# Which engine scales the first corner of the interpolated tiles while the next image's offsets are computed

## The reference, cut to what matters

```python
def _modulated_dcn(x, w_off, b_off, w):
    om = conv(x, w_off) + b_off          # 27 channels: 18 offsets, 9 masks
    ...
    v = samp(y0, x0) * ((1 - ly) * (1 - lx))[:, None] + samp(y0, x0 + 1) * ((1 - ly) * lx)[:, None] \
        + samp(y0 + 1, x0) * (ly * (1 - lx))[:, None] + samp(y0 + 1, x0 + 1) * (ly * lx)[:, None]
    v = v * mask[:, None]
    return jnp.einsum('bckhw,ock->bohw', v, w.reshape(w.shape[0], C, KK))
```

## Time and profile before

| | |
|---|---|
| median of 3 runs | 5400.81 us (5400.7 to 5404.68) |
| profiled execution, its own time | 5390.38 us |
| its span | 5388.6 us |
| granted TensorE clock, mean | 0.972 of full speed |
| TensorE matmul busy | 4889.6 us |
| VectorE busy | 4392.5 us |
| ScalarE busy | 2297.6 us |
| GpSimd busy | 2282.9 us |

### The profile page before, as it was taken

One profiled execution on the slowest core, in us unless ns is written; L12 is line 12 of the kernel. 1 busy time (PEld: TensorE's weight loads), 2 busy tenths in 40 slices (PEclk: granted clock), 3 DMA queues, 4 the chain that ended last, 5 costly groups with the idle time before them and its releaser, 6 DMA issues. The chain is left out here.

```text
span 5388.6 us, 80437 instructions
## 1 busy us (share of the span) xinstructions
PE 4889.6 (91%) x26816; PEld 2678.9 (50%) x26816; DVE 4392.5 (82%) x11212; ACT 2297.6 (43%) x5430; POOL 2282.9 (42%) x2311
## 2 busy tenths in 40 slices
PE   7868999999989998999989999899998989988888
PEld 4435554555545555455544555445554555544443
DVE  5656888878887888878888788888888878898998
ACT  2234444344443443534445344343444444443554
POOL 0003444444453444434444444444444344454776
PEclk9979999999999999999999999999999999999999
DMA  4326778877798777977779777887778877788999
GB/s 162 122 93 208 271 248 291 304 250 264 247 318 285 251 266 245 337 269 259 257 251 338 250 258 256 277 315 250 275 254 292 297 252 263 251 305 308 387 398 353
DMA packets 493125, 1451.51 MB, mean 269 GB/s; under 512 B 47396, under 2 KB 117420, under 8 KB 492460
## 3 DMA queue, kind: packets, MB, share of 16 engines
q0 software_dynamic: 331776, 1208.11, 64.3%
q1 hardware_dynamic: 160940, 238.27, 12.6%
HBM read 1309.60 MB, written 136.59 MB: 268 GB/s over the span
## 5 line engine op out<-in xcount | busy, mean ns | idle before, releaser
L730 POOL DMA_INDIRECT G<-table,IDX x2304 | 2282.0, 990 | 3066.6 <-DVE V L1381 2269.6
L749 PE MATMUL ps<-VT,s_wconv 128*128 128x512 f32 x4608 | 2277.5, 618 | 39.7 <-DVE R L1165 39.7
L1381 DVE SCALAR_TENSOR_TENSOR V<-G,WT,V 128x256 f32<-128x256 f32 x4608 | 2019.1, 479 | 122.6 <-DVE V L1381 3.2
L1109 ACT ACTIVATE VT<-ps 128x512 f32<-128x512 f32 x1152 | 686.0, 595 | 2390.0 <-PE ps L955 2387.9
L749 PEld LDWEIGHTS ps<-VT,s_wconv 128*128 128x128 f32 x4608 | 828.7, 194 | 871.7 <-issue 836.1
L1374 DVE SCALAR_TENSOR_TENSOR V<-G,WT 128x256 f32<-128x256 f32 x2304 | 1006.5, 477 | 84.0 <-ACT G L1098 40.1
L1129 DVE TENSOR_TENSOR E<-ps,s_band 128x512 f32<-128x512 f32 x1024 | 649.5, 682 | 455.3 <-PE ps L811 273.3
L955 PEld LDWEIGHTS ps<-s_ident,V 128*128 128x128 f32 x4608 | 574.5, 143 | 755.8 <-issue 754.5
L1098 ACT ACTIVATE G<-G,WT 128x256 f32<-128x256 f32 x1850 | 841.2, 499 | 111.0 <-DMA G<-table,IDX 110.1
L955 PE MATMUL ps<-s_ident,V 128*128 128x128 f32 x4608 | 708.8, 277 | 86.4 <-DVE V L1381 84.4
L787 PE MATMUL ps<-XN,s_wqk 128*128 128x512 f32 x1024 | 490.1, 606 | 14.8 <-ACT XN L1011 14.6
(11 more groups left out here) (101 smaller groups left out, 2764.9 us busy)
## 6 DMA issues: line engine op xcount, KB each, us to landing
table<-E SPq DMA_DIRECT2D x384, 176.0 KB
G<-table,IDX POOLq DMA_INDIRECT x2304
X<-in_x SPq DMA_DIRECT2D x64, 512.0 KB, 7.3
x<-X SPq DMA_DIRECT2D x64, 512.0 KB, 7.0
R<-x SPq DMA_DIRECT2D x64, 512.0 KB
out<-R SPq DMA_DIRECT2D x64, 512.0 KB, 5.8
G<-in_x SPq DMA_DIRECT2D x56, 512.0 KB, 4.4
s_wconv<-in_wconv SPq DMA_DIRECT2D x1, 2304.0 KB, 9.2
```

What stands on the lines that cost most here:

```text
L730: e.indirect_dma_start(G[a % NG][:, :], None, T[b % 2], bass.IndirectOffsetOnAxis(ap=IDX[b % 2][:, col:col + 1], axis=0)).then_inc(d_g[a % ...
L749: mm = e.matmul(CV[oh][:, :], s_wconv[:, h, t, oh * P:(oh + 1) * P], VT[U % 2][:, h, :], start=(t == 0 and h == 0), stop=(t == 8 and h == 1))
L1109: e.activation(VT[U % 2][:, :, 2 * P * pair:2 * P * (pair + 1)], BK[banks.place[use]][:, :].rearrange("p (h n) -> p h n", h=2), ACT.Copy). ...
L1381: e.scalar_tensor_tensor(vt[:, :], gt[:, q * C:(q + 1) * C], wt[:, col, q:q + 1], vt[:, :], ALU.mult, ALU.add).then_inc(lerp[q - 1], 1)
```

## The change

Every "scale" step is ScalarE's. The flag, the state that set it and the count of scales by engine go, as does VectorE's multiply with its semaphore. VectorE's first lerp waits for ScalarE's count alone.

```diff
     def front(b):
-        offsets_run[0] = False
         yield from layer0(b)
-        offsets_run[0] = True
         yield from offset_phase(b)
-        offsets_run[0] = False
...
         def scale(m):
             if m < PAIRS:
-                steps.append(("scale", b, m, not offsets_run[0]))
+                steps.append(("scale", b, m))
...
-                elif kind == "scale" and s[3]:
+                elif kind == "scale":
                     b, m = s[1:3]
...
                     for a, gt, vt, col in pairs:
-                        if not scaled[a][0]:
-                            e.wait_ge(d_g[a % NG], 16 * (a // NG + 1))
-                            if u % 9 == 0 and pair == 0:
-                                e.wait_ge(wts, WTS * (b * NCH + c + 1))
-                            e.tensor_scalar(gt[:, 0:C], gt[:, 0:C], wt[:, col, 0:1], None, ALU.mult).then_inc(dve_scale, 1)
                     if M > 2:
                         e.wait_ge(*filled(("vt", M - 3)))
...
                     for a, gt, vt, col in pairs:
-                        on_act, count = scaled[a]
-                        if on_act:
-                            e.wait_ge(act_scale, count)
-                        else:
-                            e.wait_ge(dve_scale, count)
+                        e.wait_ge(act_scale, a + 1)
                         e.scalar_tensor_tensor(vt[:, :], gt[:, C:2 * C], wt[:, col, 1:2], gt[:, 0:C],
                                                ALU.mult, ALU.add).then_inc(lerp[0], 1)
```

More of the change, by code:

```diff
@@ L88, in order_of_steps @@
     have_kv, have_logits, have_x1 = set(), set(), set()
-    offsets_run = [False]
     def hop(n):
@@ L402, in runs @@
     return [(0, slot, n)] + ([(n, 0, 4 - n)] if n < 4 else [])
[L405 to L414, removed]
 def build(nc, x, wqk, wv, wn, wkx, bkg, alpha, beta, wproj, woff, boff, wconv,
@@ L421, in build @@
     banks, prods = rotations(steps)
-    scaled = scale_counts(steps)
     ctx = ExitStack()
@@ L530, in build @@
         wts = sem("wts")
-        dve_scale = sem("dve_scale")
         lerp = [sem(f"lerp{q}") for q in range(1, 4)]
@@ L1355, in _ @@
                     pairs = [(2 * M + i, G[(2 * M + i) % NG], V[(2 * M + i) % NV], (4 * c + 2 * pair + i) * 9 + t) for i in range(2)]
-                    for a, gt, vt, col in pairs:
-                        if not scaled[a][0]:
-                            e.wait_ge(d_g[a % NG], 16 * (a // NG + 1))
-                            if u % 9 == 0 and pair == 0:
-                                e.wait_ge(wts, WTS * (b * NCH + c + 1))
-                            e.tensor_scalar(gt[:, 0:C], gt[:, 0:C], wt[:, col, 0:1], None, ALU.mult).then_inc(dve_scale, 1)
                     if M > 2:
```

## The result

The changed kernel takes **5449.4 us** (median of 4 runs, 5448.2 to 5450.9) against 5401.3 us before: +48 us, a ratio of 1.0088 with a 95% interval of 1.0074 to 1.0101. A second comparison in later runs gave 1.0095 (1.0078 to 1.0112). The forecast was 5434 us, in a range of 5409 to 5450.

The account below looks back on a forecast made before the run. TensorE was taken as the bound in the stretches. Terms 28.4 - 0.4 + 5 = 33 us brought the profiled 5390.4 to 5423.5; the median's 10.4 us difference gave 5434 us, 8-in-10 range 5409 to 5450.

Parts of the forecast that it names:

- the stretches: Seven parts beside the first seven images' convolution where VectorE's scales stood: six of about 160 us, the last 119 us.
- the two waits of the earlier trace: TensorE's waits for ScalarE's copies of the offsets' logits (LS, 24 times, 22.4 us) and normalized input (XN, 12 times, 6.9 us).
- The main term, 36 x 0.79 = 28.4 us: A product pair delays each of 36 awaited ScalarE copies by 0.79 us, priced from layer 0; bounds 0 and 36 us.
- 1.52 us in hand: Third chunk's logits copy ends 1.52 us before TensorE needs it, so a 0.79 us delay there stays covered.
- VectorE's relief, zero: VectorE losing 142.3 us of products gains nothing before the tail; bounds 0 and 32.6 us.
- Gathers, zero: ScalarE needs gathered tiles two pairs earlier but adds no waits; bound a few waits of at most 1.7 us.
- the exponential, zero before the tail: VectorE's waits for ScalarE's Exp grow by up to 0.79 us each, covered by finished lerps; cost taken as nothing.
- The tail's -0.4 us: End of the last stretch: Exp 0.79 us later, two pairs of VectorE's scales gone at 0.61 us each, net -0.4 us.
- The clock, +5 us: Longer TensorE waits bring three more falls to lower clock, about 1.7 us each; between none and 41 us.
- (a): Rival: VectorE's load holds TensorE back at the stretches' exits, so the change is faster: 5367 us; chance 5%.
- (b): Rival: no change, the 36 delays are taken back later or ScalarE reaches the products early: 5401 to 5411 us; 10%.
- (c): Rival: late exponentials use up VectorE's lead in each chunk, TensorE waits for lerps inside stretches: about 5475 us; 5%.

Follow-up runs that it names:

- the filled version: Changed kernel plus six identity matmuls on TensorE ahead of each of the 36 waits for LS and XN (ScalarE's copies): 5434.4 us, 1.0064.
- `r_before`: The kernel before the change, run again unchanged for its trace on the comparison chip: 5400.0 us, 0.9996.
- `r_change`: The changed kernel, run again unchanged on the comparison chip: 5449.9 us, 1.0095 against the kernel before.
- `e3_left_out`: Kernel before, with VectorE's 454 scales left out and nothing in their place: 5396.9 us, 0.9992.
- `e4_ahead`: Changed kernel, but during the offsets' steps each pair's scale step stands ahead of the turn, not behind it: 5399.5 us, 0.9993 against the kernel before.
- `r_ahead_all`: Changed kernel, with every scale step of images 0 to 6 ahead of the turn, beside layer 0 too: 5345.3 us, 0.9904 against the kernel before.

## Why the prediction was right

**The bound and the reading of the waits.** Right. TensorE was the bound in the stretches, and each added microsecond of its idleness stands at the two waits of the earlier trace rows that the prediction named.

**The main term, 36 x 0.79 = 28.4 us.** Measured 26.9 us by the waits, 27.1 by TensorE's idle time, and about 27 by the filled version. The price read from a look-alike in another part of the same trace held to 0.01 us at the place of the earlier trace rows; over the 36 places the delay is 0.68 to 0.80 us. ScalarE's share of the stretches rose to 53%, not to about 60%: that figure was added up from full durations. That 1.52 us in hand would cover a delay of 0.79 was right too: the number of the waits stayed 24 and 12.

**VectorE's relief, zero.** Right: -0.08% with the scales left out and the rest as it was, within the interval. At the end of the first stretch VectorE stands still for TensorE 4.88 us (5.37 before), and the waits for V are the same 32 us.

**Gathers, zero, and the exponential, zero before the tail.** Right: no wait of ScalarE for a gather before 4995 us; VectorE's waits for the Exp doubled and stayed behind TensorE's lead. The tail's -0.4 us did not show: TensorE's wait there is 5.29 us and was 4.97. Its size can't be told from the falls of the clock there.

**The clock, +5 us.** This term was mis-sized, and it is what the forecast lacks of the measured 48. The price of a fall, 1.7 us, was about right (1.65 measured). The number was not: I took three more falls "as a judgement", and there were 12 more between the first two traces and 14 between `r_before` and `r_change`; TensorE's busy time in the stretches grew by 21 us. For the same reason the stretches are 7 us longer each and not the 4 us that the prediction gave as its sign. The prediction noticed the direction and had the upper bound of 41 us in its text, but it had no count behind the three. Counting the waits elsewhere in the trace of before would not have given one either. Between the stretches a fall follows, within 2 us, 23 of the 51 waits of 1.7 to 2.1 us and 5 of the 31 of 1.3 to 1.7 us. At the lengths that the 36 waits took on, 11 of 1.96 us and more and 18 of 1.3 to 1.7, these shares make 8 falls, and 10 if the long ones are taken like the waits for the scores' logits (14 of 21): three to five more than before, near what I had judged. There were 17. The sign that the stretches are another case was in the trace: at 1.18 to 1.24 us 5 of their 11 waits were followed by a fall, and none of the 15 waits of 0.9 to 1.3 us between them. So the measured time lies within the range only by 0.6 us, and it does so because the range's upper end left room for more falls than the sum had. As far as the clock goes that is luck; the mechanism and its main term are no luck.

**Rivals.** (a), VectorE as the bound, fell with `e3_left_out`. (b), a delay taken back later, fell: the stretches are longer by the waits and the falls, and nothing came back. (c), TensorE waiting for V inside a stretch, did not occur. The rule of the Trainium skill, "ScalarE: Activation LUTs", section "Rules for kernel authors", to put a plain multiply on VectorE and not on ScalarE, points the right way for this change, but for another reason than the one it gives, the time for each element. The same products on ScalarE are free, or part of a gain of 1%, where they stand ahead of the evacuation (`e4_ahead`, `r_ahead_all`).

## What to carry to other kernels

When work moves to an engine with idle time, ask what stands behind it in that engine's queue, and on which of these results the bound engine stands at that moment; the share of busy time says nothing about it. Put the moved work in front of the instruction for which the engine waits anyway, not behind it, as long as its inputs are there by then. When waits of TensorE grow, a lower clock behind them can cost as much as the waits. Count falls at the very places that will grow, and where that gives no number, carry the term as a range from none to one fall at each wait; a share counted at other places gives about half of what came here.

## What the runs showed of the hardware that I had not expected

The lower clock weighs as much as the idleness ahead of it. 17 falls cost 28 us in `r_change`, and `r_ahead_all`, with 31 fewer falls and the same idle time, is 50 us less busy. How many waits are followed by a fall is not told by their length: of the waits of 1.7 to 2.1 us outside the stretches and ahead of the last image it was 22 of 51 in `r_before` and 1 of 22 in `r_ahead_all`. Outside the stretches, with nearly the same waits, there were 53 falls in one kernel and 69 in another that differs from it by 36 short fillers elsewhere, and these parts took 19 us longer. One chip ran the same kernel before 2.4% slower than the others (5529 against 5401 us), and the gain from the earlier place was larger on it, 1.3% and not 1.0%, though the two intervals touch (0.9846 to 0.9889 and 0.9888 to 0.9921).
